# Graph layer and expert feed-forward on one core: expert weights read in place by TensorE at register addresses, instead of copied by VectorE first

## The reference

```python
# x: (3125, 256); layer 1
h = layernorm(x)
agg = segment_sum(h[src], dst);  deg = segment_sum(1, dst)
x = x + h @ W_self + (agg / max(deg, 1)) @ W_neigh + b
# layer 2, per token t (xn = layernorm(x))
logits = xn @ gate_w + gate_b;   vals, idx = top_k(logits, 2);   w = softmax(vals)
f_e    = relu(xn @ w1[e] + b1[e]) @ w2[e] + b2[e]
y      = xn + sum_k w[k] * f_idx[k]
x      = x + layernorm(y) * gamma + beta
```

## Time and profile before

| | |
|---|---|
| time, median of 3 runs | 930.67 us (928.03 to 931.82) |
| the profiled execution | 929.28 us, its span 927.0 us |
| granted TensorE clock, mean over the span | 0.746 of full speed |
| busy: TensorE matmul / weight load | 539.6 us (58%) / 434.4 us (47%) |
| busy: VectorE | 551.1 us (59%) |
| busy: ScalarE | 296.6 us (32%) |
| busy: GpSimd | 605.4 us (65%) |
| gather stage | to about 610 us |
| expert stage | about 665 to 856 us |
| tail | from there to 927 us |

### The profile page before, as it was taken

One profiled execution on the slowest core, in us unless ns is written; L12 is line 12 of the kernel. 1 busy time (PEld: TensorE's weight loads), 2 busy tenths in 40 slices (PEclk: granted clock), 3 DMA queues, 4 the chain that ended last, 5 costly groups with the idle time before them and its releaser, 6 DMA issues.

```text
span 927.0 us, 15136 instructions
## 1 busy us (share of the span) xinstructions
PE 539.6 (58%) x4348; PEld 434.4 (47%) x4348; DVE 551.1 (59%) x1472; ACT 296.6 (32%) x699; POOL 605.4 (65%) x590
## 2 busy tenths in 40 slices
PE   0023456555565556656555566533699999999610
PEld 0012334434343444434444344323589999998400
DVE  8813355566655566564554554478467777775494
ACT  2701121111212112100010000010289989997522
POOL 2067777777777777777777777406757777776012
PEclk9995577676657666676666666755899999999855
DMA  7444555655655555544444444310142222224986
GB/s 185 137 130 146 156 161 167 182 177 176 189 174 175 171 164 169 150 127 125 129 122 126 124 125 129 94 51 0 53 106 93 87 92 88 77 79 105 205 152 83
DMA packets 64943, 120.09 MB, mean 130 GB/s; under 512 B 11567, under 2 KB 39391, under 8 KB 64892
## 3 DMA queue, kind: packets, MB, share of 16 engines
q0 software_dynamic: 29472, 72.56, 27.8%
q1 hardware_dynamic: 35272, 46.48, 17.6%
q10 hardware_dynamic: 148, 0.43, 0.2%
HBM read 100.21 MB, written 21.19 MB: 131 GB/s over the span
## 4 chain that ended last, share of the span: by engine, by line
POOL 45%; PE 21%; issue 15%; DVE 10%; DMA 6%; ACT 1%; POOLq 0%; ACTq 0%; SPq 0%; DVEq 0%
POOL arena L592 43%; PE PS L956 9%; PE PS L968 8%; DMA arena<-h_tab,arena 2%; PE PS L944 1%; DMA arena<-xh_tab,tok_of 1%; PE PS L933 1%; DVE arena L1374 1%; DVE W L1075 1%; DVE W L1370 1%; DVE W L1365 1%; DMA W<-z_tab 1%; DMA W<-in_dst 1%; DVE W L1358 1%; POOL AGG L608 1%
## 5 line engine op out<-in xcount | busy, mean ns | idle before, releaser
L592 POOL DMA_INDIRECT arena<-h_tab,arena x416 | 417.2, 1003 | 161.0 <-issue 159.5
L836 PE MATMUL PS<-arena 128*128 128x257 f16 x416 | 143.5, 360 | 236.0 <-DMA arena<-h_tab,arena 235.9
L836 PEld LDWEIGHTS PS<-arena 128*128 128x128 f16 x416 | 51.4, 124 | 274.3 <-issue 190.7
L837 PE MATMUL PS<-arena 128*128 128x256 f16 x416 | 146.3, 366 | 0.0
L1107 DVE TENSOR_TENSOR arena<-iota,arena 128x512 f16<-128x512 f16 x104 | 70.3, 692 | 50.8 <-PE PS L837 41.6
L1148 DVE TENSOR_TENSOR AGG<-AGG,PS 128x384 f32 x52 | 28.9, 555 | 118.5 <-PE PS L843 111.4
L956 PE MATMUL PS<-arena,AGG 128*128 128x128 f16 x1536 | 97.4, 220 | 1.8 <-DVE AGG L1324 1.8
L968 PE MATMUL PS<-AGG,arena 128*128 128x256 f16 x768 | 95.6, 273 | 0.2 <-DVE arena L1335 0.2
L707 ACT ACTIVATE arena<-PS 128x257 f32<-128x257 f32 x52 | 19.8, 380 | 231.7 <-PE PS L837 231.7
L697 ACT ACTIVATE arena<-arena 125x256 f16<-125x256 f32 x25 | 10.4, 417 | 255.4 <-DVE arena L1177 255.4
L626 POOL DMA_INDIRECT z_tab<-arena,meta_of x64 | 71.2, 1112 | 31.5 <-issue 17.9
(11 more groups left out here) (197 smaller groups left out, 995.4 us busy)
## 6 DMA issues: line engine op xcount, KB each, us to landing
W<-in_L_ffn_w SPq DMA_DIRECT2D x31, 512.0 KB, 4.1
arena<-h_tab,arena POOLq DMA_INDIRECT x416
W<-z_tab SPq DMA_DIRECT2D x3, 1344.0 KB
arena<-h_tab SPq DMA_DIRECT2D x25, 125.0 KB
arena<-in_x SPq DMA_DIRECT2D x25, 125.0 KB
out<-arena SPq DMA_DIRECT2D x25, 125.0 KB
xh_tab<-arena SPq DMA_DIRECT2D x25, 125.0 KB
out<-W POOLq DMA_DIRECT2D x3, 672.0 KB, 6.9
```

Of the source, the lines that this page charges most:

```text
L592: g.indirect_dma_start(msg[:, s, u, 0:2 * D], None, h_tab[:, :], bass.IndirectOffsetOnAxis(ap=srcT[:, t:t + 1], axis=0)).then_inc(gathered ...
L836: t.matmul(p, oh[:, h, u, :], msg[:, s, u, D:2 * D + 1], start=first, stop=False)
L837: return t.matmul(p[:, 0:D], oh[:, h, u, :], msg[:, s, u, 0:D], start=False, stop=last)
```

## The change

TensorE reads the expert number of the item itself, once in `up` and once in `down` (`pe.value_load`), and takes the weights straight out of `W1` and `W2` at an address that depends on this register (`bass.ds(e, 1)`). VectorE's two big copies, their wait for `l2_done` and the slots `w1e` and `w2e` are gone; it still copies the bias, and `w1_copied` now counts that for ScalarE. SyncE's wait ahead of the later blocks of `out` goes from the last copy to the last `down`.

```diff
--- before.py
+++ after.py
@@ -527,7 +527,7 @@
...
-            sp.wait_ge(w2_copied, NITEM)
+            sp.wait_ge(l2_done, NITEM + 2)
             for q in range(2, NT):
                 xb_load(q)
...
@@ -947,25 +947,25 @@
             def up(s, m):
 
                 n = 4 * m + s
-                pe.wait_ge(w1_copied, n + 1)
+                e = pe.value_load(items[0:1, bass.ds(n, 1)], min_val=0, max_val=NEXP - 1)
                 pe.wait_ge(x16_copied, n + 5)
                 pe.wait_ge(relu_done, n + 1)
                 for c in range(FC):
                     terms = [(wa, xa, k) for wa, xa in ((0, 0), (0, 1), (1, 0)) for k in range(KC)]
                     for y, (wa, xa, k) in enumerate(terms):
-                        ins = t.matmul(p_h[s % 2][:, c * P:(c + 1) * P], w1e[:, s % 2, wa, k, c * P:(c + 1) * P],
+                        ins = t.matmul(p_h[s % 2][:, c * P:(c + 1) * P], W1[:, bass.ds(e, 1), wa, k, c * P:(c + 1) * P].rearrange("p e f -> p (e f)"),
                                        xT[:, s % 2, xa, k, :], start=(y == 0), stop=(y == len(terms) - 1))
                 ins.then_inc(l1_done, 1)
 
             def down(s, m):
 
                 n = 4 * m + s
-                pe.wait_ge(w2_copied, n + 1)
+                e = pe.value_load(items[0:1, bass.ds(n, 1)], min_val=0, max_val=NEXP - 1)
                 pe.wait_ge(h_split, n + 3)
                 pe.wait_ge(yo_ready, n + 1)
                 terms = [(h, wa, c) for h, wa in ((hh, 0), (hh, 1), (hl, 0)) for c in range(FC)]
                 for y, (h, wa, c) in enumerate(terms):
-                    ins = t.matmul(p_y[s % 2], h[:, s % 2, c * P:(c + 1) * P], w2e[:, s, wa, c, :],
+                    ins = t.matmul(p_y[s % 2], h[:, s % 2, c * P:(c + 1) * P], W2[:, bass.ds(e, 1), wa, c, :].rearrange("p e d -> p (e d)"),
                                    start=(y == 0), stop=(y == len(terms) - 1))
                 ins.then_inc(l2_done, 1)
 
@@ -1320,13 +1320,7 @@
                 e = dve.value_load(items[0:1, bass.ds(n, 1)], min_val=0, max_val=NEXP - 1)
                 dve.wait_ge(l1_done, n + 1)
                 dve.wait_ge(relu_done, n + 1)
-                v.tensor_copy(b1e[:, s % 2, :], b1T[:, bass.ds(e * FC, FC)])
-                v.tensor_copy(w1e[:, s % 2, :, :, :].rearrange("p a k f -> p (a k f)"),
-                              W1[:, bass.ds(e, 1), :, :, :].rearrange("p e a k f -> p (e a k f)")).then_inc(w1_copied, 1)
-                if not (isinstance(m, int) and m == 0):
-                    dve.wait_ge(l2_done, 4 * (m - 1) + s + 3)
-                v.tensor_copy(w2e[:, s, :, :, :].rearrange("p a c d -> p (a c d)"),
-                              W2[:, bass.ds(e, 1), :, :, :].rearrange("p e a c d -> p (e a c d)")).then_inc(w2_copied, 1)
+                v.tensor_copy(b1e[:, s % 2, :], b1T[:, bass.ds(e * FC, FC)]).then_inc(w1_copied, 1)
```

## The result

| | before | changed |
|---|---|---|
| time, median (lowest to highest) | 931.03 us (928.03 to 931.82, 4 runs) | 1051.71 us (1050.42 to 1053.09, 4 runs) |
| ratio | | 1.1318 [1.1289, 1.1347] |
| span of the profiled execution | 927.0 us | 1049.7 us |
| first matmul of `up` to last of `down` | 664.8 to 856.2: 191.4 us | 667.5 to 976.3: 308.8 us |
| from there to the end | 70.9 us | 73.4 us |

The kernel is 13% slower. Of the 122.7 us by which the span grew, 117.4 lie in the stage, 2.7 ahead of its first matmul of `up` and 2.5 behind it. The same two kernels, measured once more on another chip, gave 1.1317 [1.1281, 1.1353] (929.16 and 1050.83 us).

The account below looks back on a forecast made before the run. TensorE's array bounds the expert stage at 2.90 us per item; afterwards its sequencer does, at T = A+B+C+D+E = 5.39 us per item. Stage +155.6 and end +3 us, so 744.3 + 64 T gives 1089 us, range 1020 to 1165.

Parts of the forecast that it names:

- A: Two value loads per item on TensorE's sequencer, 0.63 us each with pauses: 1.27 us per item, upper end 1.71.
- B: 24 address steps per item on TensorE's sequencer, 16 in `up` and 8 in `down`, 0.105 us each: 2.52 us.
- C: 24 weight loads of `up` and 12 matmuls of `down` addressed by a register, 0.04 us each: 1.44 us per item.
- D: The event wait before each transpose group (L940) on TensorE's sequencer: 0.11 us per item, there before and hidden.
- E: 44 static instructions per item on TensorE's sequencer, 1 ns each: 0.05 us.
- The waits that move: `up` and `down` wait on a sequencer instruction for semaphores written a period before in the steady part: 0 us.
- The end: SyncE's loads of later blocks of `out` wait for the last `down`, making VectorE's first tail addition late: +3 us (0 to 6).
- The pause once more: Rival: each register-addressed instruction costs TensorE's sequencer the 60 ns pause, 0.05 to 0.07 us; 6.11 us per item, 1135 us; chance 0.23.
- "dear" addressing: Rival: register-addressed instructions cost 0.08 us or more, or loads also stay at 484 ns; from 1180 us up; chance 0.10.
- "Cheap" addressing: Rival: register-addressed instructions on TensorE cost 0.01 us or less each; at most 1020 us, 1000 as value; chance 0.06.
- The clock: Rival: TensorE's clock falls to 1.2 GHz in the expert stage, about 5.8 us per item, 1115 us; chance 0.12.
- Not slower: Rival: the sequencer's extra work stays hidden behind the array, about 2.2 us per item; 932 us; chance 0.03.

Follow-up runs that it names:

- The last experiment: The kernel before with 16 increments of an unused semaphore per item added on TensorE, all in `up`: ratio 1.0281, item 3.31 us.
- the experiment on the wait: The changed kernel with SyncE's wait ahead of the later blocks of `out` for the last `up`, not the last `down`: ratio 1.0749, last `down` to end 71.7 us.

## Why the prediction was right or wrong

**What bounds the kernel before: right.** The copies lay beside the bound; with them gone and nothing put on TensorE the time stays within 1%. That was run on chips with the stalls only; on one without them the copy of `W2` alone was taken out, at 1.003.

**The sequencer becomes the bound: right, and the array starves behind it.** The forecast of 1089 us came out 3.6% too high, with 1051.7 inside the range. By the forecast's own 744.3 + 64 T, the measured T of 4.82 gives 1052.8. The sum was right, and T = 5.39 was not. Its terms:

- A, loads: 1.27, measured 1.29. TENSOR_LOAD took 299 to 301 ns where 264 was expected from VectorE's, and the second part 151 instead of 165. The 484 ns of the earlier trace rows was no measure of a repeated load.
- B, 24 plain address steps of 0.105: 2.52, measured 24 x 0.104 = 2.50.
- **C, 36 register-addressed instructions at 0.04: 1.44, measured 0.48. This is the step that failed**, though at 0.013 each it stayed inside my own 0.01 to 0.05. I had read 0.025 from VectorE as the price of a register in an instruction, raised it to 0.04 for TensorE's longer pause and multiplied it by 36. What the rows show is a price per address step, 20 ns beyond instruction and pause, however many matmuls follow; matmuls of fixed address after an increment cost 40. I read it as the hand-over from the sequencer's own instruction to what follows. Counted per step, even VectorE's 0.025 (which there is per pair of address and copy) would have given 24 x 0.025 = 0.6, and T 4.55. The row was of use, and it was multiplied by the wrong count.
- D, event waits: 0.11, measured 0.34. I counted L940 alone. One wait of `up` (L952) and one of `down` (L965) are rows of their own as well, and they were so in the kernel before, where I had not looked. They cost a step each even when the semaphore was long there. So the change did not make these rows, as "now wait on an ISA row" suggests; it made the sequencer's time count.

```profile
L952 PEldq EVENT_SEMAPHORE  x64: 51/51/1154, 664.4 to 848.9; - x64
...
L965 PEldq EVENT_SEMAPHORE  x64: 51/51/371, 671.5 to 854.5; - x64
```

- E, static instructions: 0.05, and no row shows such a share.
- Not foreseen: longer steps, 0.21 us an item.

Errors in C and D had opposite signs (-0.96 and +0.23); with the longer steps and E they leave the 0.57 us that T was too large, 36 us in the stage. That the forecast came as near as 3.6% is in part luck: with C right and the rest as it was, T would have been 4.43 and the forecast 1028, 2.3% too low.

**The waits that move: priced at 0, and right for this change.** Of other engines TensorE waited in the stage only for DVE L1329, once, for 0.7 us (and once for a gather to land, 1.5 us). The last experiment shows that this is no general rule: with the copies kept, `w1_copied` became late.

**The end: +3 us forecast, +2.5 measured**, and the experiment on the wait agrees. The stage's first matmul came 2.7 us later, and 64 x 4.82 + 0.3 is the 308.8 of the stage; I had put 2 us for both.

**The rivals.** "The pause once more" would make T 6.11, and "dear" addressing 6.8 and more: neither is there, and three matmuls between two address steps cost what one does. The Trainium skill's page "TensorE: Matmul & The Clock Gate" (section "Wait — 56ns, not 53.3ns?") has some 62 ns for a matmul in the sequencer's microcode, with hardware decode off; that isn't what a register address brings here, where 36 such instructions add 0.48 us in all, 13 ns each. The estimate of 2.23 us put that price on the 24 weight loads too, for which the section gives none. "Cheap" addressing (T up to 4.31) was closest in its reason, since a register in the matmul showed no price of its own, but it left out the 20 ns per step, the two waits and the longer steps. The clock stayed at 1.00 with 2.9 of 4.8 us streamed. "Not slower" fell: the sequencer's steps, pauses included, follow one another through the whole item.

Of the signs that I named, the period with "issue" in it, addresses of 37 to 50 ns in steps of 0.10 to 0.19, the clock and the missing waits came as said. The matmuls of `up` stand 0.090 us apart (2.15 for 24), not 0.11, TENSOR_LOAD is 14% longer than 264 ns, VectorE's busy time fell by 82 us and not 90, and 3% of the address steps were longer than said, up to 0.28 us.

## What to carry to other kernels

Where TensorE is the bound with short matmuls (56 ns each), price what runs on its sequencer like work. Here it was about 0.12 us for each address step, 0.64 for a value load, 0.11 for each wait that stands by itself; those waits are in the trace of the kernel before, hidden, and have to be counted too. Here a copy of 0.70 us on an engine with slack bought off 16 steps of 2 us on the engine without. Reading in place is harmless only if that sum stays under the array's time per item, as with `down` alone (1.003), and if the part that it stretches does not close a loop of waits, as the increments in `up` did. Even then it wins nothing while the array is the bound.

## What the runs showed of the hardware that was not expected

- Three to four times an item a step of TensorE's sequencer is 30 to 155 ns longer (0.154 to 0.279 us instead of 0.124), some 0.23 us an item in all, with the same lengths recurring in the kernels that have address steps (0.154, 0.182, 0.215, 0.279). In the changed kernel they lie 1.0 to 1.7 us apart. What they are was not tried.
- An event wait or an increment takes 51 ns on TensorE's sequencer and 0.106 to 0.111 us as a step, with matmuls between 0.126 to 0.170; an address instruction 46 ns and 0.124 with matmuls between.
- The same kernel (`down` alone in place) took 1049 us on one chip and 932 on another, with the gathers ending 67 us later and holes on ScalarE in the expert stage. The cause of that is open; the stage of the changed kernel, paced by TensorE's sequencer, was the same on both kinds to 0.3 us.
